# Two graph layers on one core: each of the three stationaries of a message tile made by two Vector products instead of one

## The reference

```python
x_j = node_features[col]
m = jnp.einsum('ei,ej,ijh->eh', x_j, edge_attr_e3nn, W_msg_tp) * norm_msg_tp
m = jax.nn.silu(m)
m = m @ W_msg_lin * norm_lin
agg = jax.ops.segment_sum(m, row, num_segments=n_nodes)
```

## Time and profile before

| | |
|---|---|
| Median of 3 runs | 5913.23 us (5909.15 to 5915.31) |
| The profiled execution | 5915.26 us |
| Its span, first to last instruction | 5913.5 us |
| Granted TensorE clock, mean | 0.899 |
| Vector (DVE) busy | 5183.5 us (88%) |
| TensorE (PE) busy | 4496.4 us (76%) |
| GpSimd (POOL) busy | 4372.5 us (74%) |
| ScalarE (ACT) busy | 2455.9 us (42%) |
| L722, the three products, 588 instructions | 399.9 us, 680 ns each |
| L707, the one-hots, 1568 instructions | 633.1 us, 425 ns each |
| L654, the gathers of the first loop, 1568 instructions | 1683.2 us, 1073 ns each |
| L688, waiting for gathers, 196 instructions | 240.3 us busy, 451.8 us idle before them |

### The profile page before, as it was taken

The page is one execution under the profiler, slowest core; times in us unless marked ns, Lnnn a source line. Parts: engine busy times, 40 slices in busy tenths (PEclk is TensorE's granted clock), DMA queues, the critical chain, the costliest instruction groups (busy, mean ns, idle before and its releaser), DMA issues. The chain is left out here.

```text
span 5913.5 us, 71022 instructions
## 1 busy us (share of the span) xinstructions
PE 4496.4 (76%) x17923; PEld 2168.9 (37%) x17923; DVE 5183.5 (88%) x8909; ACT 2455.9 (42%) x4460; POOL 4372.5 (74%) x4105
## 2 busy tenths in 40 slices
PE   1178887887878878678888888888888888888880
PEld 1044444444444444333333333333333333333330
DVE  5378787787877878699999999999999999999996
ACT  1022222222222222155555555555555555555553
POOL 6677777777777777277777777777777777777762
PEclk6599999999999999889999999999999999989995
DMA  4133333333333333111111111111111111111113
GB/s 134 47 92 92 96 96 93 99 92 94 87 77 77 76 78 76 30 26 27 27 27 27 27 27 27 27 27 27 26 26 27 27 27 27 27 27 27 27 21 114
DMA packets 335266, 315.22 MB, mean 53 GB/s; under 512 B 190903, under 2 KB 274576, under 8 KB 334977
## 3 DMA queue, kind: packets, MB, share of 16 engines
q0 software_dynamic: 156096, 199.34, 14.9%
q1 hardware_dynamic: 179137, 115.52, 7.2%
HBM read 220.82 MB, written 168.57 MB: 66 GB/s over the span
## 5 line engine op out<-in xcount | busy, mean ns | idle before, releaser
L1020 POOL DMA_INDIRECT xg<-x1tab,edge x1920 | 1976.2, 1029 | 585.2 <-issue 583.7
L787 PE MATMUL pagg<-ohh,stt 128*128 128x512 bf16 x4704 | 1702.6, 401 | 458.9 <-DVE ohh L707 458.7
L654 POOL DMA_INDIRECT bg<-btab,mt x1568 | 1683.2, 1073 | 479.6 <-issue 476.3
L1091 PE MATMUL ps<-work,ident 128*128 128x512 f32 x3840 | 1942.7, 630 | 0.2 <-DVE work L1179 0.2
L788 PE MATMUL pagg<-ohh,stt 128*128 128x270 bf16 x4704 | 1370.9, 291 | 0.0
L1140 DVE TENSOR_TENSOR work<-pw,xg 128x1024 f32<-128x1024 f32 x960 | 1112.5, 1210 | 21.3 <-DMA xg<-x1tab,edge 21.3
L1080 PE MATMUL pw<-w,et 99*128 99x512 bf16 x1920 | 680.1, 441 | 574.3 <-DVE work L1140 568.5
L1091 PEld LDWEIGHTS ps<-work,ident 128*128 128x128 f32 x3840 | 779.6, 203 | 725.4 <-issue 632.3
L1063 ACT ACTIVATE work<-work,mt 128x256 f32<-128x256 f32 x1920 | 861.5, 500 | 131.3 <-DVE work L1140 109.2
L787 PEld LDWEIGHTS pagg<-ohh,stt 128*128 128x128 bf16 x4704 | 481.5, 102 | 1140.6 <-DVE ohh L707 535.6
L750 ACT CAST joined<-rest 128x256 bf16<-128x256 f32 x196 | 79.7, 407 | 1572.6 <-DVE rest L677 1572.6
(11 more groups left out here) (232 smaller groups left out, 3780.5 us busy)
## 6 DMA issues: line engine op xcount, KB each, us to landing
etab<-joined SPq DMA_DIRECT2D x389, 102.0 KB, 2.3
xg<-x1tab,edge POOLq DMA_INDIRECT x1920, 2.4
bg<-btab,mt POOLq DMA_INDIRECT x1568
rtab<-zrow SPq DMA_DIRECT2D x56, 384.0 KB, 3.3
tab<-rtab SPq DMA_DIRECT2D x7, 2048.0 KB, 8.3
e<-in_edge_attr_dram SPq DMA_DIRECT2D x392, 32.0 KB, 2.1
e<-in_edge_attr_dram SPq DMA_DIRECT2D x392, 16.0 KB
mt<-meta SPq DMA_DIRECT2D x240, 6.0 KB
```

The lines of the kernel that those rows point to most:

```text
L654: g.indirect_dma_start(bg[:, h, i, :], None, btab, bass.IndirectOffsetOnAxis(ap=mt[:, h, 0, i:i + 1], axis=0)).then_inc(gathered[h], 16)
L787: pe.matmul(pagg[:, 0, :], w, ohh[:, h, i, 0:CUT], start=False, stop=False, skip_group_check=True)
L1020: g.indirect_dma_start(xg[:, b % 4, i, :], None, x1tab, bass.IndirectOffsetOnAxis(ap=edge[:, b, i, EW - 1:EW], axis=0)).then_inc(x_in[b % ...
L1091: pe.matmul(ps[:, b % 2, :], ident[:, :], work[:, b % 4, i, :, :, :].rearrange("p i a o -> p (i a o)"), start=i == 0, stop=False)
```

## The change

In `stationaries`, each product over all 8 slots is written as two products over 4 slots each. The first half covers slots 0 to 3, the second slots 4 to 7; the semaphore `stt_done` goes up once, on the second. Operands, types, places in the order and buffers stay as they are.

```diff
--- before.py
+++ after.py
@@ -719,10 +719,12 @@
                             part = (s1, s2, s3)[i - 3]
                             if i == 5:
                                 v.wait_ge(s3_done, k + 1)
-                            v.tensor_tensor(stt[:, h, i - 3, :, :, :],
-                                            part[:, h, :, :].unsqueeze(2).to_broadcast([LANES, J, LO, D]),
-                                            ohx[:, h, :, :, :],
-                                            ALU.mult).then_inc(stt_done, 1)
+                            for lo in range(0, J, J // 2):
+                                some = slice(lo, lo + J // 2)
+                                ins = v.tensor_tensor(stt[:, h, i - 3, some, :, :],
+                                                      part[:, h, some, :].unsqueeze(2).to_broadcast([LANES, J // 2, LO, D]),
+                                                      ohx[:, h, some, :, :], ALU.mult)
+                            ins.then_inc(stt_done, 1)
 
                 messages(0, 0, 0)
                 with v.Fori(0, NBLK // B4 - 1) as t:
```

## The result

The changed kernel took 5930.6 us (median of 8 runs, 5927.5 to 5937.0), the kernel before 5910.8 us (8 runs): a ratio of 1.0034, 95% interval 1.0023 to 1.0045. It is 20 us slower. Forecast was 5824 us; the measured time lies outside the range of 5800 to 5900 and on the other side of the kernel before.

What follows compares the result with a forecast made beforehand. GpSimd's chain of 1568 gathers was taken to bound the first loop. Shorter holds on seventh and eighth gathers gain 196 x 0.463 = 91 us, less one for filling: 5824 us, range 5800 to 5900.

Steps and rivals of the forecast that it cites:

- GpSimd's chain sets the pace: First loop: 1568 gathers at 1.073 + 0.306 us make up the whole loop, 2162 us.
- Vector's 0.20 us per tile are hidden: L722 products: splitting costs Vector 0.067 us per pair, 39 us over 196 tiles, all within its 2.29 us slack.
- The wait at L688: Vector's wait for a tile's last gather to land: a sign, down from 449 to about 320 us.
- The next half begins 0.13 after the gather, too late to hold it: Seventh gather of a tile: held only by the running one-hot, it ends at 1209.30 instead of 1209.82.
- rows 8 and 9: Second loop's trace rows: a gather ended 0.82 after the first of three chained operations, the next beginning 0.10 after it.
- The other begins 0.13 after the gather: Eighth gather of a tile: held only by the running half, it ends at 1210.63 instead of 1211.10.
- the halves act as one: Rival, L722's second pair: gather waits until both halves are through, 0.20 us per tile, 39 us slower, 5954; chance 0.12.
- partly held: Rival, seventh gather: the half beginning 0.13 after it holds it; gain only 0.13 per tile, 25 us, 5889; chance 0.12.
- The next tile starts from the same positions: Tile boundary: L688 begins about 1.8 after the eighth gather ends, so the next tile starts 0.46 us earlier.
- The range: Whole kernel: 5800 to 5900 us, its lower end called a third more than the sum; faster 0.82.
- the sum: First loop: 196 tiles x 0.463 us gained on seventh and eighth gathers, 91 us.

Runs made afterwards that it cites:

- h4_apart_store: The kernel before with six product halves, one-hots between all but the last two, and a tile's two stores issued ahead of its feature loads: 5838.1 us, 0.9876.
- g4_apart: The same six halves as the changed kernel, but with a one-hot between any two except the last two, against the kernel before: 5863.2 us, 0.9912.
- h1_first_only: The kernel before with only the first of the three products split, where gathers set the pace: 5916.8 us, 1.0008.
- j2_first_quarters: The kernel before with the first product in four quarters of 256 elements, the others whole: 5938.9 us, 1.0038.
- j1_f32_pair: The kernel before with only the second product split, its halves reading the f32 rest instead of the bf16 copy, where gathers set the pace: 5994.9 us, 1.0133.
- h2_wait_between: The changed kernel with the second half of the second product waiting for the first, where gathers set the pace: 5876.4 us, 0.994 of the kernel before.
- e4_first_only: The kernel before with only the first product split, on a chip where TensorE sets the pace: 0.9993 of the kernel before.
- f4_first_only: The kernel before with only the first product split, repeated on a chip where TensorE sets the pace: 1.0002 of the kernel before.

## Why the prediction was wrong, point by point

- **GpSimd's chain sets the pace**: right. The change of its mean gather times 1568 is the change of the kernel, in the changed kernel (20 of 20 us) and in h4_apart_store (1568 x 0.0486 = 76 us against 74 measured), and relieving TensorE left the order of the kernels as it was.
- **Vector's 0.20 us per tile are hidden**: right in size (0.33 from half to half, 414 ns each) and in that they cost nothing: g4_apart has them and is 50 us faster than the kernel before on its chip. The wait at L688 was to fall to 320 us; it is 436, since the gathers didn't get shorter.
- **"The next half begins 0.13 after the gather, too late to hold it"**: this is the step that failed. It was taken from rows 8 and 9, where a gather began during a product and the next product began 0.10 after it. The seventh gather begins during a one-hot. At the boundary from a one-hot into a product it isn't let in, at 0.07, at 0.14 (h1_first_only), nor at 0.27 in j2_first_quarters, bf16 or f32 (j1_f32_pair); so the seventh gather took 1.71 us where the prediction had 1.04. The rows of before had the case at 0.07 only, and I took distance for what it depends on and not the kind of the operation in front. The trace of before could have told: two of its gathers began 0.20 and 0.21 before a product, during a one-hot, and were held through the product, as this one, 0.82 past its end:

```profile
268.74 1.71 POOL L654 DMA_INDIRECT bg<-btab,mt  x1 [0.30 <-issue]
```

```profile
268.61 0.42 DVE L707 TENSOR_SCALAR ohh<-iota_hi,hilo 128x782 bf16<-128x782 f16 x1
268.94 0.68 DVE L722 TENSOR_TENSOR stt<-s,ohx 128x1024 bf16<-128x1024 bf16 x1
```

- **"The other begins 0.13 after the gather" for the eighth**: the case of a gather that begins during a half with another half 0.13 or more behind it. In h2_wait_between all 151 such gathers were let in between the halves, at 1.02 to 1.03 us, and all 15 in e4_first_only and f4_first_only, at 1.03 to 1.16; so that part of the reading held. (In j2_first_quarters, gathers that began 0.10 before the next quarter came in one boundary later, at 1.20 us, so 0.10 is about the edge.) It didn't come about, since the seventh gather was late.
- **The rival "the halves act as one"**, at 0.12: its price was right, 0.20 us per tile, 39 us, against 192 ns and 38 us. Its ground, that like operations back to back hand the hold over, explains at most the second step: the first boundary at which the gather was held lies between unlike operations, and there h1_first_only holds it with no pair behind it; and the 151 gathers above were let in between like halves. Why a gather that has waited since the one-hot is passed over there too stays open; a wait between the halves opens it (h2_wait_between). It missed the total, 5954 for 5931.
- **The rival "partly held"**, at 0.12: right that the half at 0.13 holds the gather, wrong that it is let in behind that half (1.37 us; it took 1.71).
- **"The next tile starts from the same positions"**: failed. The landing isn't a constant 1.8: in the trace of before it lies between 1.56 and 2.79 us, and its mean went from 1.83 to 1.71 and gave 19 us back through the third gather. This term was not in the sum at all.
- **The range**: its lower end, 5800, is about a quarter more gain than the sum (115 us against 91), not a third.
- **The order of the halves** decided more than their number: 5931 us side by side, 5863 with one-hots between them.

The Trainium skill's rule (SBUF — State Buffer, "SBUF: two separate sides"), an exclusive lock held for the whole instruction, agrees with gathers that end a fixed 0.82 us after an instruction. That a waiting gather is passed over where one instruction follows another, as here from one-hot to product and from half to half behind it, is more than the rule says.

## What to carry to other kernels

Where GpSimd's descriptor work sets the pace and Vector has slack, look at which Vector operation stands next to which: a gather that begins during a one-hot shortly before a product (up to 0.21 us here) was held through all products that follow without a gap, so shorter instructions help only with something else between them, or a gap. A row read as evidence must match the case in the kind of both neighbours, not only in its times. And a phase that moves by 0.1 us can move the landing of the transfers behind it: check what else is issued there before calling it constant.

## What the runs showed of the hardware that I had not expected

- A gather already waiting was passed over at the boundary from a one-hot into a product and from half to half behind it, up to 1.7 us (two bf16 halves) or 2.17 us (two f32 halves) in all, while one-hot to one-hot let it in (1.03 us; all 309 gathers that began 0.08 to 0.15 before the next one-hot where gathers set the pace). At 0.05 to 0.21 before the product none of 1658 got in where gathers set the pace, and 68 of 834 on the chips where TensorE did; at 0.25 to 0.29 it depended on the place. What makes the difference stays open.
- The same kernel took 5911 us on some chips and 7186 on others, with TensorE's products 0.7 us or more apart. What makes a chip do so stays open. There the halves with one-hots between them were 1.0 to 1.4% slower than the kernel before, and 0.9% faster in g4_apart.
- The mean landing of a tile's last gather moved between 1.71 and 1.92 us, with the position of the sync engine's stores and loads among other things; where the stores were issued 0.6 to 1.2 us before the gather's end it was 2.04 us in g4_apart.
